# Level-0 attention in batches of eight query tiles, with the probabilities turned by VectorE in 32x32 blocks

## The reference, cut to what matters

```
y = einsum('bnd,hde->bhne', x, Wkqv) + bkqv        # keys 128, queries 128, values 8 wide
A = einsum('bhnd,bhmd->bhnm', q, k) / sqrt(128)
A = softmax(where(tril, A, -inf))                  # 2048 x 2048 for each of 16 heads
sa = einsum('bhnm,bhmd->bnhd', A, v).reshape(B, N, 128)
return sa @ Wp + bp
```

## Time and profile before

| | |
|---|---|
| time, median of 3 runs | 2808.73 us (2806.97 to 2810.7) |
| profiled execution, first to last instruction | 2804.1 us |
| opening | up to 30 us |
| attention loop, first half | about 30 to 377 us |
| attention loop, second half without scans | 377 to 767 us |
| attention loop, second half with scans, and its end | 767 to 1160 us |
| transformer | 1160 to 2804 us |

### The profile page before, as it was taken

The page is one execution under the profiler, slowest core; times in us unless marked ns, Lnnn a source line. Parts: engine busy times, 40 slices in busy tenths (PEclk is TensorE's granted clock), DMA queues, the critical chain, the costliest instruction groups (busy, mean ns, idle before and its releaser), DMA issues. The chain is left out here.

```text
span 2804.1 us, 75305 instructions
## 1 busy us (share of the span) xinstructions
PE 2620.9 (93%) x29942; PEld 1739.0 (62%) x29942; DVE 2279.7 (81%) x2918; ACT 1958.5 (70%) x4022; POOL 1699.9 (61%) x1621
## 2 busy tenths in 40 slices
PE   8999999999999999798998999999999999999997
PEld 5555556565665666565665666666666666666665
DVE  6777765675577777789985889989998999899994
ACT  4455555555666666477776888888888888888884
POOL 1000002000266666577766889989999999899992
PEclk9999999999999999999999999999999999999999
DMA  3000000000011112102012111211221221111111
GB/s 93 1 1 1 1 1 3 1 1 11 4 46 46 46 45 46 38 10 90 14 29 66 30 34 31 62 45 35 59 38 37 40 61 36 28 30 36 29 27 37
DMA packets 139208, 90.35 MB, mean 32 GB/s; under 512 B 65219, under 2 KB 135855, under 8 KB 137327
## 3 DMA queue, kind: packets, MB, share of 16 engines
q1 hardware_dynamic: 138863, 85.54, 12.8%
HBM read 60.61 MB, written 6.03 MB: 24 GB/s over the span
## 5 line engine op out<-in xcount | busy, mean ns | idle before, releaser
L587 PE MATMUL ps<-xnT,qp 128*128 128x512 f32 (+3 forms) x1280 | 525.4, 541 | 17.2 <-ACT prob L814 16.3
L1841 DVE TENSOR_TENSOR rot<-ps,tab 128x2048 f32<-128x2048 f32 x192 | 430.4, 2282 | 61.3 <-ACT sq L1621 34.9
L822 ACT ACTIVATE probT<-ps 128x512 f32<-128x512 f32 (+3 forms) x384 | 207.9, 541 | 351.9 <-PE ps L600 351.8
L814 ACT ACTIVATE prob<-ps,ebias,shift 128x1024 f32<-128x1024 f32 (+7 forms) x384 | 360.4, 955 | 123.9 <-DVE ebias L704 60.3
L587 PEld LDWEIGHTS ps<-xnT,qp 128*128 128x128 f32 x1280 | 231.2, 190 | 272.5 <-issue 227.3
L1352 PE MATMUL ps<-wqk,xcT 128*128 128x512 f32 x768 | 355.7, 605 | 28.5 <-DVE area L1907 23.0
L2028 POOL TENSOR_TENSOR rot<-rot,rn 128x1024 f32<-128x1024 f32 x192 | 370.0, 1948 | 7.5
L1442 PEld LDWEIGHTS ps<-wvo,area 128*128 128x128 f32 x3072 | 353.7, 193 | 26.8 <-issue 20.9
L1442 PE MATMUL ps<-wvo,area 128*128 128x128 f32 x3072 | 360.4, 276 | 3.3 <-ACT area L1670 3.3
L695 DVE TENSOR_REDUCE nmx<-ps 128x1 f32<-128x1024 f32 (+7 forms) x256 | 245.6, 986 | 106.7 <-PE ps L587 91.9
L1663 ACT ACTIVATE ps<-ps,nmxl 128x64 f32<-128x64 f32 x1536 | 322.6, 345 | 3.7 <-DVE nmxl L1821 3.6
(11 more groups left out here) (269 smaller groups left out, 5026.0 us busy)
## 6 DMA issues: line engine op xcount, KB each, us to landing
bc<-bc_scratch SPq DMA_DIRECT2D x128, 128.0 KB, 3.1
area<-bc_scratch SPq DMA_DIRECT2D x128, 128.0 KB, 4.0
wqk<-lwqk_dram SPq DMA_DIRECT2D x6, 1024.0 KB, 7.5
xp<-xc SPq DMA_DIRECT2D x96, 48.0 KB, 3.0
xc<-xs SPq DMA_DIRECT2D x96, 32.0 KB
wvT<-lwvT_dram SPq DMA_DIRECT2D x6, 512.0 KB, 8.5
wo<-lwo_dram SPq DMA_DIRECT2D x6, 512.0 KB, 9.2
xc<-xs SPq DMA_DIRECT2D x96, 31.8 KB
```

The costliest lines, as they stand in the source:

```text
L587: mm = E.matmul(ps[:, 2 * r + o // 512, 0:w], k.qp[:, group % 2, g % NTH * P:(g % NTH + 1) * P], k.xnT[:, k0 + o:k0 + o + w], start=True, ...
L814: A.activation(k.prob[:, r, 0:nk], ps[:, 2 * r:2 * r + 2, :].rearrange("p a b -> p (a b)")[:, 0:nk], ACT.Exp, bias=k.ebias[:, row % 2:row ...
L1841: V.tensor_tensor(k.rot[:, n % 2, w, :, :].rearrange("p c (h d) -> p c h d", d=DH), bcast(heads(what, n), 1, 2), bcast(k.tab[:, n % FRAME, ...
```

## The change

The loop's unit becomes a batch: eight query tiles of one head against 1024 keys. There are 48: `(h, 0, 0)`, first half, with a causal edge; then for each head `(h, 1, 0)`, second half against keys 0 to 1023 ("square"), and `(h, 1, 1)`, second half against keys 1024 to 2047, again with the causal edge. There are 384 pieces as before, of the same sizes. In a step of the second half (two pieces) the two pieces were parts of one row; now they are neighbours in a batch.

- The maximum of a piece is its own, kept in `mneg`; the two parts of a row are weighed and added at the end (`part_shares`, `weights`, `combine`), on POOL and ACT.
- DVE turns `prob` itself, in 32x32 blocks within each 32 partitions, into `probT` in SBUF. The copies L713 and L822 and the matmuls L600 and L605 go.
- The value products of a whole batch run during the next batch, 128 matmuls of 32 rows x 32 columns over up to 256 queries (8 tiles of 32), into banks 4 to 7; three batches share the 32 columns. After three batches ACT copies four banks, PE gathers with eight matmuls, ACT copies again.
- Each partition strip needs every key block's values, so the values go to DRAM (32 DMAs) and come back four times for each batch (192 DMAs).
- Queries are evacuated by ACT, expert products by ACT and then gated and summed by POOL (six instructions a tile). They are computed into the second bank of the pair of a piece of at most 512 keys, and `pair_free` waits for their copies too; visits take a pair of banks of their own, in turn with the pieces. DVE's mask addition of the first half becomes a bf16 matmul.
- SBUF areas are laid out anew; layer 0's transformer weights are loaded at step 46 of the second half and no longer at the start.

```diff
+BATCH = [(h, 0, 0) for h in range(H0)] + [(h, 1, part) for h in range(H0) for part in range(2)]
+TURNS = [list(range(b, min(b + 3, H0))) for b in range(0, H0, 3)] + [list(range(b, min(b + 3, NB))) for b in range(H0, NB, 3)]
...
+def shares(b):
+    return (5, 5, 5, 5, 6, 6) if is_square(b) else (2, 4, 5, 6, 7, 8)
+def value_steps(U):
+    b, i = divmod(U, NTH)
+    if b == 0 or not 1 <= i <= 6:
+        return range(0)
+    n = shares(b)
+    return range(sum(n[:i - 1]), sum(n[:i]))
...
+    def pair_free(z):
+        what, U, i = SLOTS[z]
+        if what == "visit":
+            E.wait_ge(s("half_act"), at["act"][f"{U}{i}"])
+            return
+        E.wait_ge(s("prob"), U + 1)
+        what, n, c = beside(U)
+        if what == "queries":
+            E.wait_ge(s("qp"), 2 * n + c + 1)
+        elif what == "experts":
+            E.wait_ge(s("xe"), 2 * n + c + 1)
...
-        for c in range(min(4, nk // P)):
-            mm = E.transpose(ps[:, 4, c * P:(c + 1) * P], k.prob[:, r, c * P:(c + 1) * P], k.ident[:])
...
+        for f in steps:
+            c, i0 = f % 4, 0 if is_square(b) else f // 4
+            for q in range(4):
+                at = slice(WIN * q, WIN * (q + 1))
...
+                    of = k.probT[x][at, 0:NTH * STRIDE[x]].rearrange("p (i n) -> p i n", i=NTH)[:, i0:NTH, WIN * f:WIN * (f + 1)]
+                mm = E.matmul(ps[WIN * c:WIN * (c + 1), 4 + q, WIN * i0:WIN * NTH], k.vb[at, x, NTH * c + f // 4, VB - WIN - VW * j:VB - VW * j], of,
+                              start=j == 0 and f < 4, stop=b in LAST_OF and f >= HALF - 4, skip_group_check=True)
...
+    for z, (what, U, i) in enumerate(SLOTS):
+        if what == "piece" and U >= NTH:
+            values(U // NTH - 1, value_steps(U))
+        if z + 2 < len(SLOTS):
+            pair_free(z)
+            issue(z + 2)
+        if what == "piece" and U % NTH == NTH - 1 and U // NTH - 1 in LAST_OF:
+            gather(LAST_OF[U // NTH - 1])
...
     def turn_probs(U):
...
+        V.wait_ge(s("prob"), U + 1)
+        if i == 0 and b >= 2:
+            V.wait_ge(s("value_mm"), b - 1)
+        V.transpose(k.probT[x][:, i * STRIDE[x]:i * STRIDE[x] + nk], k.prob[:, U % 2, 0:nk]).then_inc(s("prob_turned"), 1)
...
+            S.dma_start(k.v_d[h, half].rearrange("c a n -> (c a) n"), k.valL[:, tiles, h, :]).then_inc(s("vd"), 16)
...
+            S.dma_start(k.staged[WIN * c:WIN * (c + 1), b % 2, :, :], k.v_d[h, part].rearrange("c a n -> a c n")).then_inc(s(f"staged{b % 2}"), 16)
```

More of the change, by code:

```diff
@@ L43 @@
 NTILE = L * NT
-AREA = 12388
+AREA = 24164
 SCANS = 9060
@@ L371 @@
[L371 to L399, removed]
-    if 2 <= group < H0 and g in (2, 3):
-        return "experts", group - 2, g - 2
-    if group in (2, 3) and g in (6, 7):
-        return "experts", NT - 4 + group, g - 6
-    if row >= ROWS // 2 and row - ROWS // 2 in VISITS:
-        return ("visit", *VISITS[row - ROWS // 2])
-    return None, 0, 0
@@ L409, with is_square, piece, group_of @@
-EXPERT_ORDER = [n for row in range(ROWS) for what, n, half in [filler(row)] if what == "experts" and half]
-def scanned_in(row):
-    u = row - ROWS // 2 - FIRST_SCAN
+def is_square(b):
+    return b >= H0 and BATCH[b][2] == 0
+def piece(U):
+    b, i = divmod(U, NTH)
+    h, half, part = BATCH[b]
+    return b, i, part * KB, KB if is_square(b) else (i + 1) * P
+def group_of(b):
+    h, half, part = BATCH[b]
+    return H0 * half + h
+def step_of(U):
+    V = U - FIRST
+    return V // 2 if V >= 0 and V % 2 == 0 else None
@@ new lines, with beside @@
+SLOTS = []
+for U in range(NU):
+    SLOTS.append(("piece", U, 0))
+    if step_of(U) in VISITS:
+        SLOTS.append(("visit", *VISITS[step_of(U)]))
+SLOT_OF = {U: z for z, (what, U, i) in enumerate(SLOTS) if what == "piece"}
+def beside(U):
+    b, i = divmod(U, NTH)
+    if is_square(b) or i >= 4:
+        return None, 0, 0
+    tile = b if b < 10 else 10 + (b - H0) // 2 if b > H0 and b < H0 + 12 else None
+    if i < 2 and b + 1 < NB:
+        return "queries", group_of(b) + 1, i
+    if i >= 2 and tile is not None:
+        return "experts", tile, i - 2
+    return None, 0, 0
@@ L635, in attention_pe, with gather @@
+    def gather(turn):
+        E.wait_ge(s("ot"), turn + 1)
+        for i in range(NTH):
+            mm = E.matmul(ps[:, 4, 256 + 3 * VW * i:256 + 3 * VW * (i + 1)], k.oT[:, i, :, :].rearrange("p q n -> p (q n)"), k.pick[:], start=True, stop=True,
+                          skip_group_check=True)
+        mm.then_inc(s("pick_mm"), 1)
+    queries(0, 0, ps[:, 5, :])
+    E.wait_ge(s("G"), 7)
+    queries(0, 1, ps[:, 4, :])
     E.wait_ge(s("mask"), 1)
     E.wait_ge(s("raw"), 2)
-    scores(0)
+    E.wait_ge(s("rest"), 80)
```

688 lines of the change are left out of this document (353 added, 335 removed).

## The result

The changed kernel takes 2845.9 us (2838.8 to 2851.4), against 2809.7 for the kernel before on the same chip. The ratio is 1.0127, with an interval of 1.0107 to 1.0147. The forecast was 2769 us, faster, with a range of 2700 to 2838. It is slower by 36 us, outside the range.

What follows compares the result with a forecast made beforehand. The prediction took PE to bound the loop, with DVE and POOL's ring next where scans run. First half -33, second half without scans -17, with scans +8 and loop end +2 sum to -40 us: 2769 us, range 2700 to 2838.

Steps and rivals of the forecast that it cites:

- the sentence on the DMAs: Value saves in the loop: about 1 us each on 16 engines, all 32 over by some 70 us, nobody waiting.
- Rival (d): Saves in the first half: small writes cost 60 ns each, 123 us in all, giving 2825 us; chance 0.05.
- The values' price: New value products on PE over the 48 batches: 232 us with their bursts, at 14 ns per 256-column record.
- First half: First 16 batches: 19.6 us each, 2.7 of it waits, so 314 us against 347, -33 us.
- Rival (a): First two stretches: PE fills its waits better than forecast; half of the waits gone gives 2720 us; chance 0.17.
- Second half without scans: 61 steps, PE's work plus its waits: 373 us against 390, -17 us.
- With scans: 64 steps of the second half, where DVE with POOL's ring becomes the bound: 386 us against 378, +8 us.
- the ring: Scan stretch: DVE's scan, POOL's three instructions, then the next scan take 5.63 us, so no step is under 5.6.
- End: End of the loop: the last batch's products run alone, 2.8 + 0.3 us, then copies, gather and weighing; net +2 us.
- (b): Scan stretch: DVE, ACT and POOL don't interleave, a step costs 6.9 us rather than 6.0, giving 2821 us; chance 0.17.
- (c): Value products: 32x32 tiles run no faster than four strips, 27.5 ns a record, giving some 2900 us; chance 0.05.
- (e): Scan stretch: PE, waiting a fifth of the time, is granted 1.2 GHz, some +120 us, giving 2890; chance 0.04.

Runs made afterwards that it cites:

- when spread: The changed kernel with the same 32 saves of 36-byte packets, two to a batch over the first 16 batches in place of two bursts: 2766.3 us.
- the split above: The changed kernel, bursts kept, but batches 2 to 15 take the values staged for batches 0 and 1, so none waits for late staging: 2800.2 us.
- doubling: The kernel with wide saves, with every value product made twice into the same sum: 3105.8 us.
- wide saves: The changed kernel with values laid out by head in SBUF, each save 128 packets of 288 bytes in place of 1024 of 36: 2759.3 us.
- the saves in pairs: The changed kernel with its 36-byte packets, but SyncE waits after each two saves until both have landed: 2865.8 us.

## Why the prediction was wrong

**The step that failed** is the sentence on the DMAs: they "wait for nobody", a save "takes about 1 us on 16 engines", and the 32 "are over by some 70 us". The 16 ns from the earlier trace rows are an engine's time in a quiet queue, and there small packets do look that cheap (9.9 ns when spread). What limits a save is how fast its packets land, 4.2 to 5.0 ns each over all in this kernel, 4.3 to 5.1 us a save where I had 1. So the 32 saves and what stood between them took from 27.5 to 170 us, and the staging for batch 2 was issued at 154 us, not 70. By the split above this wait is 46 to 49 us of the loss, and the rest of what lies before the first scan, 28 us, is the bursts' harm to a PE stream that needs many instructions, a term that the forecast does not have. Rival (d) had the right place and nearly the right length, 123 us for the saves, with 0.05; but its price was right by luck, since the 60 ns of the earlier trace rows are an engine's time for a packet of 1 KB, and it lacked the second part.

**The values' price** (232 us) was low. Busy time is 298.6 us, 67 more, and doubling gives 346 as an upper bound. That is most of why PE got lighter by 74 us and not by 170. The bursts of one batch with the edge, in a quiet stretch of the changed kernel:

```profile
325.35 0.66 PE L679 MATMUL ps<-area,vb 32*32 32x256 f32 x16
...
327.05 0.66 PE L679 MATMUL ps<-area,vb 32*32 32x256 f32 x32
...
328.98 1.14 PE L679 MATMUL ps<-area,vb 32*32 32x224 f32 x40
...
331.59 1.04 PE L679 MATMUL ps<-area,vb 32*32 32x192 f32 x48
...
334.32 0.95 PE L679 MATMUL ps<-area,vb 32*32 32x128 f32 x56
...
337.17 0.80 PE L679 MATMUL ps<-area,vb 32*32 32x64 f32 x64
337.90 0.49 PE L605 MATMUL ps<-xnT,qp 128*128 128x128 f32 x2
```

Start to next start these are 0.59, 0.60, 1.06, 0.97, 0.87 and 0.73, 4.8 us against the forecast 4.6: right. The square batch's records of 256 columns are the ones that I had too low: 64 of them take 1.43 us (1170.72 to 1172.15), 22 ns each and not 14 with a start of 0.3. Shorter bursts are dearer still, 40 of them 1.22 us (363.85 less 362.63 with wide saves), and the six bursts of a square batch there sum to some 6.5 us, 25 ns a record, against 5.3. With 4.8 and 6.5 the sum is an estimated 258 us. The Trainium skill (TensorE: Matmul & The Clock Gate, Part 3: Packing small matmuls) with 10.6 times for 16 tiles gives an estimated 21 ns; the trace agrees, with 22 ns in bursts of 64. Its other rule (section "Wait — 56ns, not 53.3ns?"), starts no closer than about 25 ns, does not hold here if it is taken for records: the 64 short ones come at 0.73 / 64 = 11 ns. They are 32 matmuls of the program, and those come at 23 ns, just under it.

**First half.** With the saves cured it takes 299 us; forecast 314. A batch is 16.7 to 18.7 us (321.16 to 337.90 and 302.45 to 321.16), against 19.6. With wide saves PE idles for 12 of the 297 us, 0.8 us a batch and not 2.7. The prediction had said that its waits are wrong if that is under 1, and they are. The longer waits that I had put behind a long piece don't come, since pieces of 128 to 384 keys begin the next batch. Rival (a) was partly right here.

**Second half without scans.** 375 against the forecast 373. Right by luck, from two errors of opposite sign: dearer squares, and shorter waits (PE idles for 25 us, 3.2 us a head, where I had 6.6).

**With scans.** 380.7 against 372.7, the +8 forecast. DVE's timeline has the ring as the prediction describes it:

```profile
912.08 1.46 DVE L493 TENSOR_TENSOR_SCAN area<-area,last 128x256 f32<-128x256 f32 x2 [1.27 <-POOL area L483]
913.57 0.17 DVE L499 COPY last<-area 128x2 f32<-128x2 f32 x1
...
917.78 1.40 DVE L493 TENSOR_TENSOR_SCAN area<-area,last 128x256 f32<-128x256 f32 x2 [2.45 <-POOL area L483]
```

Steps with the edge are 5.7 us (forecast 5.6), and full square steps 6.0 (888.40 to 906.45 are three; forecast 6.2). DVE was expected over 90% busy and is at 86%. PE, 87% and not 80%, was nearer to being the bound than I said, which the doubled products show.

**End.** +2 forecast, +9 measured, +6.5 with wide saves. The last batch's 256 records, alone, take 7.7 us and not 3.1 (1178.12 to 1185.77), with PE in part at the lower clock (0.83 in 1160 to 1191 us).

```profile
1178.12 3.71 PE L679 MATMUL ps<-area,vb 32*32 32x256 f32 x108 [3.93 <-DVE area L734]
1181.99 2.44 PE L679 MATMUL ps<-area,vb 32*32 32x160 f32 x128 [0.16 <-issue]
1185.46 0.31 PE L679 MATMUL ps<-area,vb 32*32 32x32 f32 x20 [1.04 <-issue]
```

**Transformer.** Forecast unchanged, measured +14. The time goes with the granted clock. The three rows are the transformer of before, of the changed kernel, and of the saves in pairs:

```profile
1160.00:2804.00 1644.00, 1511.53 (x21350) 1049.21 (x21349) 1470.32 (x1435) 1302.58 (x2938) 1388.47 (x1345) 0.99 0.17 40
```

```profile
1191.00:2849.00 1658.00, 1523.19 (x21348) 1054.41 (x21348) 1473.40 (x1434) 1300.90 (x2938) 1388.87 (x1346) 0.98 0.16 39
```

```profile
1222.00:2868.00 1646.00, 1512.56 (x21348) 1050.51 (x21347) 1472.80 (x1434) 1300.55 (x2938) 1388.31 (x1344) 0.99 0.16 40
```

By the traces' clock record the sum of its stretches at 1.2 GHz was 41, 78 and 49 us. Over the ten single-product profiles the transformer's time follows that sum (41 to 55 us: 1642 to 1647; 59 to 68: 1650 to 1652; 74 to 78: 1655 to 1658), whatever the loop before it did. Why the changed kernels draw more of it stays open; but of the differences between two kernels in the table, up to some 10 us can come from here and are not to be read as an effect of the edit.

**Rivals.** (b) did not happen: steps are 5.9 us and not 6.9. (c) is off by the bursts above. (e) is off, the clock is 0.96 there. With the saves cured the time is 2759 against the forecast 2769, and that closeness is partly luck: the first half gained 48 us where I had 33, and the end and the transformer took 10 back where I had 2.

## What to carry to other kernels

A transfer's price is not its packets' busy share in a quiet queue: before queueing a burst, multiply the packets by the rate at which they land, not by their time on an engine, and see which wait stands behind them on the issuing engine. Make the contiguous run longer first (36 to 288 bytes gave back the whole 77 us that lay before the first scan), else spread the saves and issue what is needed soonest ahead of them. And test a suspected contention in the instruction stream that suffers from it: the same burst cost nothing in one kernel and some 28 us in the other.

## What the runs showed of the hardware

- Packets of 36 bytes from SBUF to DRAM land at 5.0 ns each over all 16 engines with 2048 under way at a time, and at 4.2 and 3.8 in bursts (the changed kernel; the kernel before with the saves added). An engine is held for a mean of 9.9 ns when saves are spread or in pairs, and of 68 in the bursts.
- Two saves as 256 packets of 288 bytes had landed 2.0 us after their issue; as 2048 packets of 36 bytes it took 10.5 to 10.9 us.
- In a full queue transfers of instructions took an estimated 2.5 us in place of 1.1, up to 6.0, and PE stood still for up to 4.0 us at a time (7.6 in the changed kernel), where it had many small instructions; its issue waits rose from 17 to 44 us with twice the products.
- DVE's scan of 256 columns takes 0.77 us with POOL idle and 1.03 with POOL's elementwise work beside it: removing a wait between them gave back 12 us of 43.
- In 32x32 tiles, 16 side by side, short records (64 columns and fewer) come at 11 ns in bursts of 64, and records of 256 columns at 22 ns in bursts of 64 and 30 ns in bursts of 40.
